# Last layer of a four-layer kernel: scores and value mix as three split fp32r terms, scores moved behind the first output round

## What is computed

```python
# layer 2: expert MLP, added to x
h = gelu(x @ W1 + b1)                          # 256 -> 1024
x = x + concat([h @ W2 + b2, h @ We[e] + be[e]])   # 192 shared and 64 expert columns
# layer 3: attention on a side input F (256 x 256 per batch)
query = x + embed[stage]                       # one value per position, over features
prob = softmax(query @ F.T)                    # 256 x 256
x = x + prob @ F
```

## Time and profile before

| | |
|---|---|
| median of 3 runs | 2069.08 us (2065.99 to 2070.23) |
| profiled execution | 2069.09 us |
| its span, first to last instruction | 2067.2 us |
| PE busy, share of span | 1900.1 us, 92% |
| DVE busy | 1500.3 us, 73% |
| ACT busy | 1192.4 us, 58% |
| POOL busy | 704.2 us, 34% |
| mean granted TensorE clock | 0.968 |

### The profile page before, as it was taken

The page is one execution under the profiler, slowest core; times in us unless marked ns, Lnnn a source line. Parts: engine busy times, 40 slices in busy tenths (PEclk is TensorE's granted clock), DMA queues, the critical chain, the costliest instruction groups (busy, mean ns, idle before and its releaser), DMA issues. The chain is left out here.

```text
span 2067.2 us, 42750 instructions
## 1 busy us (share of the span) xinstructions
PE 1900.1 (92%) x14030; PEld 1434.7 (69%) x14030; DVE 1500.3 (73%) x2206; ACT 1192.4 (58%) x2458; POOL 704.2 (34%) x719
## 2 busy tenths in 40 slices
PE   6999999999999996299999999999967999999998
PEld 4455555555555553287878787878857999999997
DVE  6778888878888885587777777777745666666664
ACT  1566666666666664246666666666654555555553
POOL 3244445444445443333333333333311111111111
PEclk8899999999999998599999999999988999999998
DMA  4455555555655552100000000000003223222221
GB/s 79 92 104 111 108 105 108 110 103 108 111 104 107 111 101 54 30 1 1 0 0 0 0 0 0 0 0 0 0 1 109 83 69 91 69 74 85 69 86 49
DMA packets 108700, 125.76 MB, mean 61 GB/s; under 512 B 31216, under 2 KB 73200, under 8 KB 108656
## 3 DMA queue, kind: packets, MB, share of 16 engines
q1 hardware_dynamic: 92272, 102.09, 24.0%
q0 software_dynamic: 15360, 22.58, 4.1%
q10 hardware_dynamic: 1024, 0.53, 0.1%
HBM read 56.41 MB, written 9.44 MB: 32 GB/s over the span
## 5 line engine op out<-in xcount | busy, mean ns | idle before, releaser
L394 DVE TENSOR_REDUCE a_top<-a_s 128x4 f32<-128x1024 f32 x256 | 310.2, 1212 | 132.3 <-PE a_s L631 131.9
L494 ACT ACTIVATE a_e<-a_t 128x512 f32<-128x512 f32 x512 | 277.9, 596 | 134.1 <-PE a_t L645 132.1
L404 DVE SCALAR_TENSOR_TENSOR a_e<-a_e,a_w_t 128x1024 f32<-128x1024 f32 x256 | 331.2, 1294 | 6.2 <-ACT a_e L494 6.2
L910 POOL TENSOR_TENSOR b_decayed<-b_table,b_mod_t 128x1024 f32<-128x1024 f32 x64 | 127.2, 2008 | 270.6 <-ACT b_mod_t L1181 263.2
L1717 ACT ACTIVATE c_hid<-c_pH,c_b 128x256 f32<-128x256 f32 x256 | 107.7, 472 | 187.7 <-PE c_pH L1780 187.3
L1341 PE MATMUL b_pS<-b_gated_t,b_decayed 128*128 128x256 f32 x768 | 188.1, 388 | 1.0
L627 PE MATMUL a_s<-a_add_m,ident_bf 128*128 128x512 bf16 x512 | 158.8, 393 | 11.9 <-POOL a_add_m L229 5.5
L660 PE MATMUL a_v<-a_e,a_v_pad 128*32 128x256 f32 x2048 | 165.3, 395 | 1.9 <-ACT a_raw L515 1.1
L1780 PE MATMUL c_pH<-c_x_hi,c_w_hi 128*128 128x256 f32 x512 | 150.1, 293 | 12.3 <-DVE c_w_lo L1682 12.1
L631 PEld LDWEIGHTS a_s<-a_st 48*128 48x128 f32 x1024 | 78.1, 189 | 112.3 <-issue 112.3
L1341 PEld LDWEIGHTS b_pS<-b_gated_t,b_decayed 128*128 128x128 f32 x768 | 139.3, 191 | 22.0 <-issue 6.6
(11 more groups left out here) (253 smaller groups left out, 5206.9 us busy)
## 6 DMA issues: line engine op xcount, KB each, us to landing
a_st<-a_split SPq DMA_DIRECT2D x768, 64.0 KB, 2.5
a_xs<-in_xT SPq DMA_DIRECT2D x32, 256.0 KB, 2.8
x_all<-in_xT SPq DMA_DIRECT2D x32, 256.0 KB, 2.7
a_r_rep<-a_r_rows POOLq DMA_DIRECT2D x32, 256.0 KB, 5.3
c_we<-in_we SPq DMA_DIRECT2D x32, 256.0 KB, 2.7
c_key_t<-in_keyT SPq DMA_DIRECT2D x32, 256.0 KB, 3.2
c_value<-in_key SPq DMA_DIRECT2D x32, 256.0 KB, 2.7
out<-c_y POOLq DMA_DIRECT2D x32, 256.0 KB, 3.2
```

The costliest lines, as they stand in the source:

```text
L394: dve.tensor_reduce(top[:, qc, half].rearrange("p (r j c) -> p r j c", r=2, j=2)[:, :, cc], ps_s[g % 2][:], AX.X, ALU.max)\
L404: dve.scalar_tensor_tensor(out=buf[:], in0=buf[:], scalar=BIG, in1=w_t[par][:, kc].unsqueeze(1).to_broadcast([P, 4, S]), op0=ALU.min, op1= ...
L494: act.activation(e[g % E_BUFS][:, 2 * r:2 * r + 2], ps_t[r][:], ACT.Exp).then_inc(exp_done, 1)
L910: ins = pool.tensor_tensor(decayed[par][:, lo:lo + cnt], table[:, lo:lo + cnt], mod_t[:, k].unsqueeze(1).to_broadcast([P, cnt, TRACES]), A ...
```

## The change

All of it is in `expert_and_final`.

- S and V become split products like H and O (`product`): the operands query, keyT, value and the transposed probabilities each get a hi and a lo buffer. Twelve fp32r products take the place of four fp32 ones.
- The hi parts are ACT copies (`high_query`, `high_key`, `high_value`; `turned` now writes the hi part of the probabilities). The lo parts are subtractions: on DVE for query and probabilities (`low_query`, `low_prob`), on POOL for key and value (`low_key`, `low_value`).
- PE's list becomes `H0 O0 S H1 O1 H2 T O2 H3 O3 V`.
- ACT's list becomes high_query, gelu 0, high_key, gelu 1, exps, gelu 2, turned, high_x, expert_high, gelu 3, high_value.
- DVE's list becomes low_query, split 0, maxima, split 1, normalize, split 2, low_prob, low_x, split 3, residual, queries, final.
- POOL's list becomes low_key, expert_low, store, low_value.
- SP's loads of expert weights, keyT and value now wait for the lo parts of the batch two before. ACT waits for all small loads once before the first gelu, in place of the first bias alone.

The diff, cut to what the text speaks of:

```diff
@@ SP: load(n, par)
-                sp.wait_ge(elo_done, n - 1)
+                sp.wait_ge(load_lo, 3 * (n - 2) + EXPERT)
...
-                sp.wait_ge(s_mm, n - 1)
+                sp.wait_ge(load_lo, 3 * (n - 2) + KEY)
...
-                sp.wait_ge(v_mm, n - 1)
+                sp.wait_ge(load_lo, 3 * (n - 2) + VALUE)
@@ POOL
+        def low_key(n, par):
+            pool.wait_ge(load_hi, 3 * n + KEY)
+            pool.tensor_tensor(key_p[par][1][:], key_t[par][:], key_p[par][0][:].bitcast(F32), ALU.subtract).then_inc(load_lo, 1)
...
         def body(n, par, ahead, splits, has_3):
             if ahead:
+                low_key(n + 1, 1 - par)
                 expert_low(n + 1, 1 - par)
             if has_3:
                 store(n - 1, 1 - par)
+            if ahead:
+                low_value(n + 1, 1 - par)
@@ DVE
+        def low_query(n):
+            dve.wait_ge(qhi_done, n + 1)
+            at_least(dve, s_mm, n)
+            dve.tensor_tensor(query_p[1][:], query[:], query_p[0][:].bitcast(F32), ALU.subtract).then_inc(qlo_done, 1)
+
+        def low_prob(n):
+            dve.wait_ge(pthi_done, n + 1)
+            at_least(dve, v_mm, n)
+            dve.tensor_tensor(prob_t[1][:], pT[:], prob_t[0][:].bitcast(F32), ALU.subtract).then_inc(ptlo_done, 1)
...
             if has_3:
-                maxima(n - 1)
+                low_query(n - 1)
             if ahead:
                 split(n + 1, 0)
             if has_3:
+                maxima(n - 1)
+            if ahead:
+                split(n + 1, 1)
+            if has_3:
                 normalize(n - 1)
             if ahead:
-                split(n + 1, 1)
                 split(n + 1, 2)
+            if has_3:
+                low_prob(n - 1)
             if splits:
                 low_x(n + 2, par)
+            if ahead:
+                split(n + 1, 3)
             residual(n, par)
             queries(n, par)
-            if ahead:
-                split(n + 1, 3)
             if has_3:
                 final(n - 1, 1 - par)
@@ ACT
+        def high_key(n, par):
+            act.wait_ge(d_key[par], landed(n, par))
+            if not (isinstance(n, int) and n < 2):
+                act.wait_ge(s_mm, n - 1)
+            act.activation(key_p[par][0][:], key_t[par][:], ACT.Copy).then_inc(load_hi, 1)
...
         def body(n, par, ahead, splits, has_3):
+            if has_3:
+                high_query(n - 1)
             if ahead:
                 hidden(n + 1, 0)
+                high_key(n + 1, 1 - par)
+                hidden(n + 1, 1)
             if has_3:
                 exps(n - 1)
             if ahead:
-                hidden(n + 1, 1)
                 hidden(n + 1, 2)
...
                 hidden(n + 1, 3)
+                high_value(n + 1, 1 - par)
@@ PE
-        def scores(n, par):
-            pe.wait_ge(query_done, n + 1)
-            pe.wait_ge(d_key[par], landed(n, par))
-            at_least(pe, exp_done, n)
+        def product(out, w, x):
             for m in range(C):
                 for k in range(C):
-                    ins = pe.matmul(pS[:, m], query[:, k, m * P:m * P + P], key_t[par][:, k], start=(k == 0), stop=(k == C - 1))
-            ins.then_inc(s_mm, 1)
+                    for i, j in ((0, 0), (1, 0), (0, 1)):
+                        ins = pe.matmul(out[:, m], w[i][:, k, m * P:m * P + P], x[j][:, k],
+                                        start=(k == 0 and i == j == 0), stop=(k == C - 1 and j == 1))
+            return ins
+
+        def scores(n, par):
+            pe.wait_ge(qlo_done, n + 1)
+            pe.wait_ge(load_lo, 3 * n + KEY)
+            at_least(pe, exp_done, n)
+            product(pS, query_p, key_p[par]).then_inc(s_mm, 1)
...
             if ahead:
                 hidden(n + 1, 1 - par, 0)
+            output(n, par, 0)
             if has_3:
                 scores(n - 1, 1 - par)
-            output(n, par, 0)
             if ahead:
                 hidden(n + 1, 1 - par, 1)
```

More of the change, by code:

```diff
@@ L1495, in expert_and_final @@
     hid_lo = [sb(f"hid_lo{i}", [P, 2, S], F32R) for i in range(ROUNDS)]
+    key_p = [[sb(f"key_{part}{i}", [P, C, S], F32R) for part in ("hi", "lo")] for i in range(2)]
+    value_p = [[sb(f"value_{part}{i}", [P, C, D], F32R) for part in ("hi", "lo")] for i in range(2)]
     query = sb("query", [P, C, S])
+    query_p = [sb(f"query_{part}", [P, C, S], F32R) for part in ("hi", "lo")]
     neg_max = sb("neg_max", [P, C])
@@ L1500, in expert_and_final @@
     prob = sb("prob", [P, C, S])
-    prob_t = sb("prob_t", [P, C, S])
+    prob_t = [sb(f"prob_t_{part}", [P, C, S], F32R) for part in ("hi", "lo")]
     y = [sb(f"y{i}", [P, C, S]) for i in range(2)]
@@ L1509, in expert_and_final @@
                                                   for n in ("d_exp", "d_bias", "d_emb", "d_key", "d_val", "stored"))
-    d_w1, d_b1, d_w2, w_hi, w_lo = (sem(n) for n in ("d_w1", "d_b1", "d_w2", "w_hi", "w_lo"))
-    xhi_done, xlo_done, ehi_done, elo_done = (sem(n) for n in ("xhi", "xlo", "ehi", "elo"))
+    d_w1, d_w2, w_hi, w_lo = (sem(n) for n in ("d_w1", "d_w2", "w_hi", "w_lo"))
+    xhi_done, xlo_done, load_hi, load_lo = (sem(n) for n in ("xhi", "xlo", "load_hi", "load_lo"))
     hid_mm, gelu_done, hhi_done, hlo_done, out_mm, x3_done = (sem(n) for n in ("hid_mm", "gelu", "hhi", "hlo", "out_mm", "x3"))
     query_done, s_mm, max_done, exp_done, inv_done, prob_done = (sem(n) for n in ("query", "s_mm", "max", "exp", "inv", "prob"))
-    t_mm, pt_done, v_mm, y_done = (sem(n) for n in ("t_mm", "pt", "v_mm", "y"))
+    t_mm, pthi_done, ptlo_done, v_mm, y_done = (sem(n) for n in ("t_mm", "pthi", "ptlo", "v_mm", "y"))
+    qhi_done, qlo_done = sem("qhi"), sem("qlo")
     def xn(n, k):
@@ L1524, in batch_of @@
         return src[bass.ds(n, 1)]
-    LOADS = 7
+    LOADS = 8
+    KEY, EXPERT, VALUE = 1, 2, 3
     block = ctx.enter_context(nc.Block())
@@ L1542, in _ @@
         sp.dma_start(w1[:], t["w1"].rearrange("(k p) e -> p k e", p=P)).then_inc(d_w1, 16)
-        sp.dma_start(b1[:], t["b1"]).then_inc(d_b1, 16)
+        sp.dma_start(b1[:], t["b1"]).then_inc(d_in, 16)
         sp.dma_start(w2[:], t["w2"].rearrange("(k p) e -> p k e", p=P)).then_inc(d_w2, 16)
@@ L1593, in expert_low, with low_value @@
         def expert_low(n, par):
-            pool.wait_ge(ehi_done, n + 1)
+            pool.wait_ge(load_hi, 3 * n + EXPERT)
             pool.tensor_tensor(w2b_lo[par][:, :, SHARED - P:P], we[par][:], w2b_hi[par][:, :, SHARED - P:P].bitcast(F32),
-                               ALU.subtract).then_inc(elo_done, 1)
+                               ALU.subtract).then_inc(load_lo, 1)
+        def low_key(n, par):
+            pool.wait_ge(load_hi, 3 * n + KEY)
+            pool.tensor_tensor(key_p[par][1][:], key_t[par][:], key_p[par][0][:].bitcast(F32), ALU.subtract).then_inc(load_lo, 1)
+        def low_value(n, par):
+            pool.wait_ge(load_hi, 3 * n + VALUE)
+            pool.tensor_tensor(value_p[par][1][:], value[par][:], value_p[par][0][:].bitcast(F32), ALU.subtract).then_inc(load_lo, 1)
         def body(n, par, ahead, splits, has_3):
             if ahead:
+                low_key(n + 1, 1 - par)
                 expert_low(n + 1, 1 - par)
@@ L1602, in body @@
                 store(n - 1, 1 - par)
+            if ahead:
+                low_value(n + 1, 1 - par)
+        low_key(0, 0)
         expert_low(0, 0)
+        low_value(0, 0)
         loop(pool, body)
@@ L1635, in queries @@
             dve.wait_ge(d_emb[par], landed(n, par))
-            at_least(dve, s_mm, n)
+            at_least(dve, qlo_done, n)
             at = slice(n * S, n * S + S) if isinstance(n, int) else bass.ds(n * S, S)
@@ L1693, in _ @@
         loop(dve, body)
+        low_query(NB - 1)
         maxima(NB - 1)
         normalize(NB - 1)
+        low_prob(NB - 1)
         final(NB - 1, 1)
@@ L1709, in expert_high @@
                 act.wait_ge(out_mm, ROUNDS * (n - 1))
-            act.activation(w2b_hi[par][:, :, SHARED - P:P], we[par][:], ACT.Copy).then_inc(ehi_done, 1)
+            act.activation(w2b_hi[par][:, :, SHARED - P:P], we[par][:], ACT.Copy).then_inc(load_hi, 1)
         def hidden(n, r):
@@ L1730, in turned, with high_value, high_query @@
             at_least(act, v_mm, n)
-            act.activation(prob_t[:], pT[:], ACT.Copy).then_inc(pt_done, 1)
+            act.activation(prob_t[0][:], pT[:], ACT.Copy).then_inc(pthi_done, 1)
+        def high_key(n, par):
[3 more added lines that the diff above has]
+            act.activation(key_p[par][0][:], key_t[par][:], ACT.Copy).then_inc(load_hi, 1)
+        def high_value(n, par):
+            act.wait_ge(d_val[par], landed(n, par))
+            if not (isinstance(n, int) and n < 2):
+                act.wait_ge(v_mm, n - 1)
+            act.activation(value_p[par][0][:], value[par][:], ACT.Copy).then_inc(load_hi, 1)
+        def high_query(n):
+            act.wait_ge(query_done, n + 1)
+            at_least(act, s_mm, n)
```

(28 more changed lines are left out.)

## The result

| | before | changed |
|---|---|---|
| median | 2067.53 us | 2115.04 us |
| range | 2064.08 to 2070.23 | 2112.85 to 2116.05 |
| profiled execution, its span | 2069.09, 2067.2 | 2114.03, 2112.3 |
| PE busy | 1900.1, 92% | 1894.2, 90% |
| mean granted clock | 0.968 | 0.967 |

The changed kernel is slower: ratio 1.0227, 95% interval 1.0204 to 1.0250, about +47 us. One execution, of 4454.62 us, took twice as long as all others: it counts in the median of four, not in the ratio or the range in the table, and the other three have a median of 2114.03. Forecast were +26.6 us and a range up to 2114. The direction was right, the size some 20 us too small; the time lies at the upper edge of the range, by the median of four 1 us outside it.

What follows compares the result with a forecast made beforehand. PE was taken to bound the kernel. Thirty bodies at 1.37 - 0.62 gave +22.5 us, start +1.7, last body +1.6, tail +0.8: together +26.6, so 2095.7 us, range 2084 to 2114.

Steps and rivals of the forecast that it cites:

- What bounds, what is saved.: PE is always busy and bounds the round; cheaper S and V save 0.62 us per body.
- T's wait.: PE before T: a chain of 5.5 us against 4.26 of cover; with the late key copy, a 1.37 us stall.
- T's own length.: The PE piece T was taken to last 0.44 us.
- "S. No stall, but only 0.15 to spare.": PE before S: low_query ready 4.1 us after O3, against 4.26 us of cover, so no wait.
- "more comes late": Rival: POOL's work makes S 0.35 us late, 2106 us; with keyT at 3.5 too, 2115; chance 14%.
- The key copy.: high_key on ACT, waiting for keyT to land, makes gelu 1 late by 0.1 us.
- POOL beside DVE.: POOL subtractions hold up DVE's low_x, which ends just when split 3 wants DVE: no loss, no spare.
- The ends.: Outside the steady rounds: start +1.7 us, last body +1.6, tail +0.8.
- Clock and table drain.: Two rivals: PE's clock falls after each stall before T, 2158 us, 5%; ACT's table switch adds 1.38 per body, 2137, 2%.

Runs made afterwards that it cites:

- early_low_query: no_collision with low_query behind final and ahead of split 3 on DVE, ACT's list unchanged; 2059.15 us, ratio 0.9957.
- scores_back: Changed kernel with S standing before O0 again, all else as changed; 2159.25 us, ratio 1.0442.
- both_small_pool: both_moves with POOL's two added subtractions cut to 8 of 256 columns from batch 2 on; 2058.31 us, ratio 0.9959.
- no_collision: both_moves with maxima before split 0 on DVE and the key copy behind gelu 1 on ACT; 2059.93 us, ratio 0.9963.
- after_small_pool: Changed kernel with POOL's two added subtractions cut to 8 of 256 columns from batch 2 on; 2118.02 us, ratio 1.0250.
- both_moves: Changed kernel with exponentials, then key copy, ahead of gelu 1; normalize ahead of split 1; residual and queries ahead of split 3; 2087.47 us, ratio 1.0096.
- mended: no_collision with low_query behind final and ahead of split 3 on DVE, and high_query ahead of high_value on ACT; 2065.49 us, ratio 0.9991.
- no_collision_waits: no_collision with PE's wait for the query's lo part last of the three before S; 2057.03 us, ratio 0.9949.
- order_only: Kernel before with the changed order of PE, ACT and DVE, keeping its fp32 products; 2116.31 us, ratio 1.0239.

## Why the prediction was half right

- **What bounds, what is saved.** Right. V 1.44, PE work of a round 14.73 (early_low_query), so 0.56 saved where 0.62 were forecast, clock 1.00 in the steady part.
- **T's wait.** 1.37 forecast, 1.40 measured. The chain's parts held: gelu 0.86, load 1.29, exponentials to T 2.02 against 1.93. That the sum fits this well is in part luck: 0.1 for the key copy was not there, and 0.09 more came behind the exponentials. Its reason was half wrong: the text named the place of S and the place of the exponentials together. With S moved back the wait stays at 1.41 (scores_back); with S behind O0 and the exponentials ahead of gelu 1 it is gone (both_small_pool, no_collision). It is the latter.
- **T's own length.** Failed: taken as 0.44, it is 0.66 after a wait. I had the row for that (0.67 in the tail) and put it down to the tail. 0.22 x 30 = 7 us.
- **"S. No stall, but only 0.15 to spare."** This is the step that failed most. From the first product of V to that of S the prediction counted 4.1 us; measured are 4.75 and 4.57 in turn, from 1964.19 to 1968.94 and from 1947.56 to 1952.13. Every handoff was put at 0.03. But split 3 starts 0.27 after V's first product; from low_query's end to S's first product it takes 0.26 and 0.25; and in one body of the pair queries to high_query takes 0.12, high_query to low_query 0.11. The instructions themselves were counted right. So S starts 0.46 and 0.28 us late, some 0.4 in the mean, 30 times: 12 us. The rival "more comes late" named the place and nearly the size (0.35), with other causes, and was given 14%.

```profile
1966.43 0.69 DVE L1656 TENSOR_TENSOR c_query<-x_all,c_embed 128x512 f32<-128x512 f32 x1
1967.24 0.64 ACT L1782 ACTIVATE c_query_hi<-c_query 128x512 fp32r<-128x512 f32 x1 [0.72 <-DVE c_query L1656]
1967.99 0.69 DVE L1662 TENSOR_TENSOR c_query_lo<-c_query,c_query_hi 128x512 fp32r<-128x512 f32 x1 [0.27 <-ACT c_query_hi L1782]
```

- **The key copy.** Put at 0.1 us late, 3 us in all; it costs nothing.
- **POOL beside DVE.** low_x ended just as split 3 was wanted, as counted (1964.40 against 1964.46). That the cast of split 0 and normalize can be blocked too was not seen. It costs nothing in the changed kernel (after_small_pool) and 29 us in both_moves.
- **The ends.** Forecast +4.1. The first O0 comes 1.7 later, exactly as forecast, but the wait before it has grown from 1.9 to 3.1 us and the clock falls: O0 takes 2.90 and the next H 2.56 us. From the first O0 to the third 2.7 us are lost. The stretch from V in the last body but one to the end took 3.1 us more instead of 2.4. Together 7.5 against 4.1.
- **Clock and table drain.** Both rivals fell: 1.00 with thirty waits of 1.4 us, and 1.29 from table load to exponentials.

The sum, by rounds: forecast 15.29 + 1.37 - 0.62 = 16.04, measured 16.72, so 0.68 missing, 20 us in thirty. Of it S is about 0.4, T's own length 0.22, the saving 0.06 and T's wait 0.03. The ends add 3.4 us to what was missed. That makes more than the 20 us by which the total is off; as the stages began 7 us apart in the profiled runs, for no reason that is shown, the total can't be closed more closely.

## What to carry to other kernels

In a software pipeline on engines that each work off a list in order, ask of every moved step which instruction its chain now starts from: putting the exponentials behind gelu 1 tied them to a product that was not theirs, and the added copies and subtractions had no part in that wait. They cost elsewhere: 0.4 us a round at S, and at T once the first wait was gone. Count handoffs as measured at that place: before S they were 0.25 us, not 0.03, so a spare of 0.15 was none, and a wait cost 0.2 more than the idle time shown. Adding POOL work to a kernel means choosing which DVE instructions it may meet: the same added subtractions cost 29 us or nothing, by their order.

## What the runs showed of the hardware

The PE clock at the start of the stage was not expected to matter. Windows of the changed kernel before and after the wait for the first O0 (length; PE, PEld, DVE, ACT, POOL busy; clock):

```profile
1559.00:1563.00 4.00, 4.00 (x34) 3.82 (x32) 2.71 (x6) 2.80 (x8) 0.00 (x0) 1.00 0.71 227
1566.00:1571.60 5.60, 5.45 (x25) 5.48 (x26) 1.12 (x2) 0.00 (x0) 2.47 (x3) 0.50 0.17 50
```

After 3.1 us of idle PE the granted clock is 0.50, the level of 1.2 GHz, for the next O0 and H; after 1.9 us in the kernel before, and after each of the waits of 1.4 us, it stayed at 1.00. The length of this wait alone doesn't decide it. Of the twelve profiles with 3.1 us, six have a first O0 of 2.90 us and six, mended and no_collision_waits among them, one of 1.6. And order_only, with the 1.9 us of the kernel before, has one of 2.52, at a lower clock:

```profile
1565.50:1568.00 2.50, 2.48 (x13) 2.50 (x14) 0.00 (x0) 0.00 (x0) 0.00 (x0) 0.59 0.40 137
```

The second thing is the size of a blocked DVE cast: 2.0 to 2.2 us for an instruction of 0.43, where it lay beside POOL's store issue (0.72) and the subtraction behind it (1.30). It ends behind the second, and it is the second that makes it long: in after_small_pool the same cast beside the same store issue, with a subtraction of 0.27 behind it, takes 0.61 to 0.66 (POOL's rows, then DVE's).

```profile
1903.30 0.73 POOL L1595 DMA_DIRECT2D out<-c_y  x1 [4.53 <-DVE c_y L1688]
1904.05 0.27 POOL L1611 TENSOR_TENSOR c_value_lo<-c_value,c_value_hi 128x16 fp32r<-128x16 f32 x1
1903.63 0.61 DVE L1641 CAST c_hid_hi<-c_hid 128x512 fp32r<-128x512 f32 x1
```
